# Copying the last tile of the transposed probabilities in the first attention: ScalarE for every other pair, or VectorE for every pair

## What is computed

```python
q = (query @ Wq + bq).reshape(B, Nq, H, D).transpose(0, 2, 1, 3)
k = (key_value @ Wk + bk).reshape(B, Nkv, H, D).transpose(0, 2, 1, 3)
v = (key_value @ Wv + bv).reshape(B, Nkv, H, D).transpose(0, 2, 1, 3)
attn = jnp.einsum('bhqd,bhkd->bhqk', q, k) * scale
attn = jnp.clip(attn, -CLAMP, CLAMP)
attn = jax.nn.softmax(attn, axis=-1)
x = jnp.einsum('bhqk,bhkd->bqhd', attn, v).reshape(B, Nq, Cq)
return x @ Wo + bo          # the caller adds this to its own x
```

## Time and profile before

| | |
|---|---|
| device time, three runs | median 731.22 us, 730.6 to 733.69 |
| the profiled execution | 732.75 us, of which the span from first to last instruction is 731.0 |
| busy in the span | TensorE 638.7 us, VectorE 391.9, ScalarE 400.2, GpSimd 242.0 |
| mean granted TensorE clock | 0.94 of full |

### The profile page before, as it was taken

One profiled execution on the slowest core, in us unless ns is written; L12 is line 12 of the kernel. 1 busy time (PEld: TensorE's weight loads), 2 busy tenths in 40 slices (PEclk: granted clock), 3 DMA queues, 4 the chain that ended last, 5 costly groups with the idle time before them and its releaser, 6 DMA issues.

```text
span 731.0 us, 15087 instructions
## 1 busy us (share of the span) xinstructions
PE 638.7 (87%) x4762; PEld 512.4 (70%) x4763; DVE 391.9 (54%) x1171; ACT 400.2 (55%) x952; POOL 242.0 (33%) x307
## 2 busy tenths in 40 slices
PE   3999889999751989998999999998696999999995
PEld 2877566666450888976878666665464999999995
DVE  5222467777643111118898745555774665566662
ACT  1454689989641333245667788686331555545442
POOL 5011455555218000001110000000044787787771
PEclk9999599999955999999999999999599999999999
DMA  6118000000086388403120010000106645555552
GB/s 146 46 31 270 7 2 2 2 2 2 1 263 214 121 282 264 149 32 85 32 53 1 8 42 1 1 2 1 32 14 170 180 141 159 155 144 148 144 143 67
DMA packets 66838, 65.11 MB, mean 89 GB/s; under 512 B 10424, under 2 KB 60373, under 8 KB 66662
## 3 DMA queue, kind: packets, MB, share of 16 engines
q1 hardware_dynamic: 62204, 58.06, 26.5%
q0 software_dynamic: 1824, 4.32, 2.3%
q10 hardware_dynamic: 2762, 2.11, 1.0%
HBM read 56.17 MB, written 8.29 MB: 88 GB/s over the span
## 4 chain that ended last, share of the span: by engine, by line
PE 69%; ACT 10%; DVE 7%; issue 5%; DMA 3%; POOL 3%; SPq 2%; DVEq 1%; POOLq 0%; ACTq 0%
ACT probs L767 4%; PE psum L1119 4%; PE psum L1106 4%; PE psum L2218 3%; PE psum L2166 3%; PE psum L2168 3%; PE psum L2167 3%; PE psum L615 3%; PE psum L629 3%; PE psum L1593 3%; PE psum L706 3%; PE psum L1615 3%; PE psum L1602 3%; DMA v_all<-in_L_ffn_W_dram 3%; PE psum L696 2%
## 5 line engine op out<-in xcount | busy, mean ns | idle before, releaser
L767 ACT ACTIVATE probs<-probs,negmax 100x361 f32<-100x361 f32 x128 | 68.9, 587 | 10.7 <-POOL probs L812 10.6
L820 DVE TENSOR_SCALAR_CACHE_REDUCE probs<-psum 100x361 f32<-100x361 f32 x128 | 60.7, 531 | 19.4 <-PE psum L696 19.4
L706 PEld LDWEIGHTS psum<-ident,probs 100*128 100x128 f32 (+1 forms) x384 | 40.4, 159 | 27.6 <-issue 20.4
L706 PE MATMUL psum<-ident,probs 100*128 100x100 f32 (+1 forms) x384 | 48.9, 266 | 11.2 <-ACT probsT L775 4.8
L1147 ACT ACTIVATE kT_all<-psum,kT_all 128x128 f32<-128x128 f32 x88 | 25.2, 369 | 51.6 <-PE psum L1106 51.6
L812 POOL TENSOR_SCALAR probs<-probs 100x722 f32<-100x722 f32 x64 | 50.5, 789 | 5.1
L2347 POOL TENSOR_TENSOR we_low<-v_all,we_high 128x512 fp32r<-128x512 f32 (+1 forms) x34 | 46.0, 1373 | 17.1 <-ACT we_high L2271 12.7
L1106 PE MATMUL psum<-kT_all,v_all 128*128 128x128 f32 x352 | 43.3, 283 | 8.5 <-DMA v_all<-in_L_ffn_W_dram 3.4
L2166 PE MATMUL psum<-xT_high,we_high 128*128 128x400 f32 x128 | 45.2, 353 | 5.5 <-DVE v_all L2411 4.1
L1106 PEld LDWEIGHTS psum<-kT_all,v_all 128*128 128x128 f32 x352 | 42.1, 198 | 11.2 <-issue 7.0
L2057 POOL TENSOR_TENSOR xT_low<-kT_all,xT_high 128x1600 fp32r<-128x1600 f32 x1 | 3.6, 3567 | 131.1 <-ACT xT_high L2034 131.1
(11 more groups left out here) (420 smaller groups left out, 1691.5 us busy)
## 6 DMA issues: line engine op xcount, KB each, us to landing
v_all<-in_L_ffn_W_dram SPq DMA_DIRECT2D x16, 1024.0 KB, 7.8
kT_all<-coefT_dram SPq DMA_DIRECT2D x18, 400.0 KB, 3.7
v_all<-in_L_ffn_Wg_dram SPq DMA_DIRECT2D x34, 128.0 KB, 2.2
v_all<-in_L_ffn_Wu_dram SPq DMA_DIRECT2D x34, 128.0 KB, 2.3
v_all<-in_L_ffn_Wd_dram SPq DMA_DIRECT2D x34, 128.0 KB, 2.3
ctx_nat<-in_ctx_dram SPq DMA_DIRECT2D x16, 192.0 KB, 2.5
xs_dram<-zeros SPq DMA_DIRECT2D x1, 2048.0 KB, 7.7
rank_rows<-rank_dram SPq DMA_DIRECT2D x18, 100.0 KB, 3.0
```

What stands on the lines that cost most here:

```text
L706: last = nc.tensor.transpose(pT_ps[0:rows[t], t, hh * NQ:(hh + 1) * NQ], probs[:, n % NPB, hh, t * P:t * P + rows[t]], ident[0:NQ, 0:NQ])
L767: last = nc.scalar.activation(row, row, ACT.Exp, bias=negmax[:, n % NPB, hh:hh + 1])
L820: last = nc.vector.tensor_scalar(probs[:, n % NPB, hh, 0:NKV], psum[0:NQ, n % 2 * 2 + hh, 0:NKV], -CLAMP, None, ALU.max, ALU.max, accum_ou ...
```

## The change

VectorE copies the last tile of both pairs, behind whatever it has to normalise or add, and ahead of the clips of quad m + 2. ScalarE's copies of the last tile are gone. Nothing else differs; the semaphores and what TensorE waits for stay as they are.

```diff
--- before.py
+++ after.py
@@ -771,10 +771,6 @@
             act.wait_ge(A0.transposed, n + 1)
             nc.scalar.activation(probsT0[n % 4][:, 0:FULL, :], pT_ps[:, 0:FULL, :], ACT.Copy).then_inc(A0.probsT_ready, 1)
 
-        def take_tail(n):
-            nc.scalar.activation(probsT0[n % 4][0:TAIL, FULL, :], pT_ps[0:TAIL, FULL, :], ACT.Copy
-                                 ).then_inc(A0.probsT_ready, 1)
-
         def finish_take(b):
             act.wait_ge(A0.attended, b + 1)
             nc.scalar.activation(oT[:, :, :], o_ps, ACT.Copy).then_inc(A0.out_taken, 1)
@@ -791,7 +787,6 @@
             if b > 0 and s == 2:
                 finish_takeT(b - 1)
             take(2 * m)
-            take_tail(2 * m)
             if b > 0 and s == 0:
                 finish_take(b - 1)
             if m + 1 < M0:
@@ -848,6 +843,7 @@
                 normalise(b - 1)
             if b > 0 and s == 3:
                 add(b - 1)
+            take_tail(2 * m)
             take_tail(2 * m + 1)
             if m + 2 < M0:
                 clip(2 * m + 4)
```

## The result

The changed kernel takes 751.73 us (median of 4 runs, 751.45 to 753.96) where the kernel before took 731.48: a ratio of 1.028, 95% interval 1.025 to 1.031, so 20.2 us more at the medians. 748.0 was forecast, 742 to 756 the range. The profiled execution took 753.96, its span is 752.2, 21.2 more than the span before.

The account below looks back on a forecast made before the run. A loop of waits from VectorE to TensorE and back, 3.87 us per quad, was to bound the attention: 0.28 + 17.34 - 0.8 = +16.8 us on the 731.22 median gives 748.0 us, range 742 to 756.

Parts of the forecast that it names:

- The loop: VectorE to TensorE and back, once per quad: clips, new copy, second transposes, scores, next clips; 3.87 us, so the longest.
- handover from VectorE to TensorE: From the end of VectorE's new copy to the second transposes' weight load: 0.06 us taken, 0.12 the other bound.
- The finish: Normalising and addition on VectorE, ahead of the new copy in one quad each per batch: 0.62 and 0.80 us added.
- The sum of the stage: Attention stage, about 75 to 200 us: slow quads 0.28, quads 2 to 30 +17.34, last quad -0.8, together +16.8 us.
- T: The weight load that starts the second transposes of a quad; it waits for both copies of the first pair.
- The slow quads: Three quads at the stage's start, at the lower clock, where TensorE itself needs 5.06 us per quad: 0.28 us added.
- ScalarE's relief: Removing 32 ScalarE copies of 0.33 us frees some 0.3 us per quad, taken up by waits and slack: nothing gained.
- What follows the stage: Everything behind the last batch's addition, transfers included, moves as a block: costed at nothing.
- The first: Rival: ScalarE bounds, so its relief makes each quad 0.27 us shorter, 8.4 us in all, 722.8 us; 3%.
- The second rival: No change: the new copy is late once, by 0.8 us, then the streams settle; 732.3 us; 3%.
- the third: Rival, half of it: normalising and adding find a place outside the loop, 1.16 us per batch is left; 739.0 us; 5%.
- The fourth: Rival: gaps in TensorE's work drop its clock to 0.5 half the time, 21 us more, 769 us; 10%.

## Why the prediction was right, step by step

**The loop.** Its four terms were 1.83, 0.43, 0.68 and 0.93; they measure 1.82, 0.47, 0.69 and 0.93. The loop was put at 3.87 and is 3.91. The mis-sized term is the handover from VectorE to TensorE. I took the 0.06 of a VectorE multiplication; it is 0.12, what ScalarE's copy showed, my upper bound. Over 28 quads that is 1.1 us.

**The finish.** Normalising was put at 0.62 and addition at 0.80: the steps are 4.54 and 4.69 beside 3.91, so 0.63 and 0.78. That they are on the loop is shown by the run that moves them: 15.94 to 16.12 for 17.05 us a batch.

**The sum of the stage.** T of quad 2 to T of quad 30 was to be 117.67 us and is 118.57 (90.12 to 208.69). The weight loads of the second transposes of the quads 30 and 31:

```profile
...
208.69 0.58 PEld L706 LDWEIGHTS psum<-ident,probs 100*128 100x128 f32 x6 [1.08 <-issue]
...
211.61 0.58 PEld L706 LDWEIGHTS psum<-ident,probs 100*128 100x128 f32 x6 [0.25 <-issue]
...
```

The last quad takes 2.92, where 2.9 was predicted and 3.74 measured before. The slow quads cost 0.40 where I had 0.28. Together 0.40 + 18.24 - 0.82 = 17.8, for a predicted 16.8. From the last T to the gate it takes 7.58 us for 7.28, and these 0.3 make up the 18.1 of the attention.

**What I costed at nothing.** ScalarE's relief: right for this kernel, as its exponentials now wait for the clamp in all 20 quads. What follows the stage: wrong as put. It "moves as a block" in its work, but took 2.7 us more in the profiled pair, 1.5 to 3.0 over all pairs of traces, with 2 to 6 us more at the low clock; what makes it longer is open. The profiled pair differs by 21.2 us, 4.4 more than the sum of 16.8: 1.0 in the loop and the slow quads, 0.3 on the way to the gate, 0.4 ahead of the attention, 2.7 behind it. The medians differ by 20.2, 3.4 more than the sum; how that divides no trace shows. So the mechanism was right and its sum 1.0 short. Most of the rest is a term put at nothing that wasn't nothing, and none of the bounds listed for the forecast was for it: that 751.73 lies in the range is owed in part to room left for other things.

**The rivals.** The first was priced at 8.4 us; had VectorE been free, less than half was to be had (3.4, with no copy at all). TensorE's wait of 0.27 was real, but ScalarE's exponentials were next in line (11 waits where there were 5): here a wait's length was an upper bound of its worth. The rule of the Trainium skill, Perfetto Trace Analysis, section "Identifying the Most-Contended Engine", picked an engine whose relief is worth half a per cent, and didn't see the loop, in which none is full. The second rival fell with the loop's length, and the third with both finishing steps. The fourth, the falling clock, did not come in either trace of this change: 1.00 in every batch at full clock. It came once in the trace with the finish behind the copies, where it cost 1 us, in some quads with one copy more, and cost 13 us over the loop with two. So its distance from the changed kernel is small, and no run says what keeps it off there. A swing between two levels, as the Trainium skill, TensorE: Matmul & The Clock Gate, section "A second HAM failure mode: psum-queue depth-cycling", describes it for another kernel, is what the traces with extra copies show; the changed kernel's, with TensorE busy 12.89 of 17.04 us, don't.

## What to carry to other kernels

Before moving work to a less busy engine, look in the timeline at where that engine stands in its own stream when the work comes due; here the copy landed behind four clips, and the scores, clips, copy and transposes closed a loop of 3.91 us per quad around engines that were all at 76% or less. The loop can be summed from start-to-start times of the trace of before, and with an in-order stream everything that stands ahead of the moved instruction counts, here another 1.41 us a batch. The place matters more than the engine: the same copies two clips earlier left the kernel within 0.2% of before.

## What the runs showed of the hardware

Longer waits of TensorE came with a second price, its clock. In the changed kernel's batches the granted clock stayed at 1.00, with TensorE busy 12.89 of 17.04 us. With the finish behind the copies it fell to 0.5 once, for 3.4 us, behind a stretch with 4.37 busy us of 6. With one more VectorE copy in the loop it fell to 0.5 for 3.4 us behind a stretch with 3.27 busy us of 6, in an execution of 761 us; three that took 764 to 767 had 14 to 27 us more at the low level (mean clocks 0.928 and 0.920 for 0.937). With two, 71 us of the attention ran at the low level. So the spread between executions of one kernel, 6 us with one extra copy, went with the clock as well.

A handover between engines took 0.12 us behind a PSUM-to-SBUF copy of ScalarE and of VectorE alike, and 0.06 behind a VectorE multiplication. The ScalarE copy costs 0.50 us for 400 columns and 0.67 for 600, but three tiles in one instruction in place of two instructions brought nothing that can be told (732.15 for 732.35 us).
